# Four chained graph layers over 16 groups: the first two and the last two groups run side by side, with new step orders on all engines

## What is computed

```python
x = _layernorm(x + _L0_gnn_ref(x, adj, ...))   # weight = adj * exp(q k^T), divided by its row sum, times v
x = _layernorm(x + _L1_gnn_ref(x, adj, ...))   # three times adj @ (x @ W) + b, relu after the first two
x = _layernorm(x + _L2_gnn_ref(x, adj, ...))   # hypergraph: H = (adj != 0), up to 512, relu, layer norm, down to 256
x = _layernorm(x + _L3_gnn_ref(x, adj, adj, ..., 128))   # attention, 8 heads of 32, scores * (adj + adj), softmax
```

## Time and profile before

| | |
|---|---|
| median of 3 runs | 1045.72 us (1045.23 to 1046.17) |
| profiled execution, first to last instruction | 1044.3 us; what lies around it is 1.4 us of the median |
| PE busy | 1010.7 us (97%) |
| DVE busy | 840.8 us (81%) |
| ACT busy | 642.8 us (62%) |
| POOL busy | 491.3 us (47%) |

### The profile page before, as it was taken

How to read it: one execution, slowest core, us unless ns; L and a number is a source line. 1 busy time by engine, 2 the same in 40 slices (tenths; PEclk the granted TensorE clock), 3 DMA queues, 4 the chain that set the end, 5 groups by cost and what they waited for, 6 DMA issues and landing times.

```text
span 1044.3 us, 21534 instructions
## 1 busy us (share of the span) xinstructions
PE 1010.7 (97%) x8292; PEld 901.9 (86%) x8292; DVE 840.8 (81%) x2246; ACT 642.8 (62%) x1739; POOL 491.3 (47%) x298
## 2 busy tenths in 40 slices
PE   9799999999999999999999999999999999998876
...
PEclk8999999999999999999999999999999999999998
...
DMA packets 15078, 39.14 MB, mean 37 GB/s; under 512 B 1792, under 2 KB 1792, under 8 KB 14848
## 3 DMA queue, kind: packets, MB, share of 16 engines
...
## 4 chain that ended last, share of the span: by engine, by line
PE 91%; DVE 4%; ACT 2%; issue 1%; POOL 1%; DMA 0%; POOLq 0%; DVEq 0%; SPq 0%
PE ps L465 83%; PE ps L775 5%; PE ps L716 1%; DVE pr L1236 1%; PE ps L702 1%; PE ps L646 1%; DVE mx L1241 1%; ACT pr L935 1%; DMA pr<-in_weights 0%; DVE x L1120 0%; POOL pr L1368 0%; DVE st L1058 0%; POOL rstd L1322 0%; DVE den L1250 0%; ACT up_high L912 0%
## 5 line engine op out<-in xcount | busy, mean ns | idle before, releaser
L1368 POOL TENSOR_TENSOR pr<-pr,den 128x1024 f32<-128x1024 f32 x64 | 132.0, 2064 | 68.7 <-DVE den L1256 68.5
L935 ACT ACTIVATE pr<-pr,mx 128x128 f32<-128x128 f32 x384 | 149.3, 407 | 6.6 <-DVE mx L1241 6.6
L1322 POOL TENSOR_TENSOR rstd<-var,neg_half 128x4 f32<-128x4 f32 (+1 forms) x84 | 74.4, 886 | 96.5 <-DVE var L1069 94.8
L1347 POOL TENSOR_TENSOR x<-x,rows 128x1024 f32<-128x1024 f32 x16 | 38.0, 2376 | 169.4 <-PE ps L465 169.4
L1074 DVE TENSOR_SCALAR x<-x,mv,rstd 128x256 f32<-128x256 f32 x256 | 90.5, 414 | 23.1 <-POOL rstd L1322 23.1
L1357 POOL TENSOR_TENSOR hv<-hv,neg_half 128x2 f32<-128x2 f32 x32 | 22.4, 701 | 161.8 <-DVE hv L1202 161.8
L1058 DVE BATCH_NORM_STATS2 st<-x 128x6 f32<-128x256 f32 x256 | 92.6, 412 | 1.9
L1236 DVE TENSOR_TENSOR pr<-ps,adjB 128x1024 f32<-128x1024 f32 x64 | 75.4, 1219 | 13.9 <-PE ps L465 13.9
L935 ACT ACTIVATION_READ_ACCUMULATOR pr<-pr,mx 128x1 f32 x384 | 78.8, 205 | 0.0
L929 ACT ACTIVATE qkT<-ps,biases 128x512 f32<-128x512 f32 x64 | 39.7, 689 | 62.7 <-PE ps L465 62.4
L1352 POOL TENSOR_TENSOR up_rest<-upT,up_high 128x1024 fp32r<-128x1024 f32 x32 | 77.7, 2430 | 0.0
...
## 6 DMA issues: line engine op xcount, KB each, us to landing
xT<-in_xT SPq DMA_DIRECT2D x16, 512.0 KB, 5.0
x<-in_x SPq DMA_DIRECT2D x16, 512.0 KB, 3.7
out_x<-x SPq DMA_DIRECT2D x32, 256.0 KB, 2.0
adjT<-in_adjT SPq DMA_DIRECT2D x16, 256.0 KB, 5.2
adjB<-in_adj SPq DMA_DIRECT2D x16, 256.0 KB, 5.0
pr<-in_weights SPq DMA_DIRECT2D x2, 512.0 KB, 6.0
qkT<-in_weights SPq DMA_DIRECT2D x1, 1024.0 KB, 11.8
...
```

Of the source, the lines that this page charges most:

```text
L935: act.activation(pr[:, b, k, :], pr[:, b, k, :], ACT.Exp, bias=mx[:, b, k:k + 1], accum_out=den[:, b, 0, k:k + 1]).then_inc(exp_ready, 1)
L1322: pool.tensor_tensor(rstd[i][:, bs], var[i][:, bs], neg_half[:, bs], ALU.pow).then_inc(rstd_ready[i], len(pairs))
L1368: pool.tensor_tensor(pr[:, b], pr[:, b], den[:, b, 1, :].unsqueeze(2).broadcast_to([P, HEADS, P]), ALU.mult).then_inc(pr_ready, 1)
```

## The change

Four things, made together.

- **Two groups side by side at both ends.** Group 1 runs its stage A beside group 0's, in tiles that stages B and C don't use yet (`begun(g)`, names ending in `_b`) and in the upper four PSUM banks (`low`). Group 15 runs its stages B and C beside group 14's, in tiles of stage A (`ended(g)`, names ending in `_z`) and in the lower four banks (`up4`). To place one tile over another, `sb` now gives out addresses itself.
- **Stage A a group further ahead.** In the loop A is group t, its last steps (`T`, from `gcn_3s` on) t-1, B t-2 and C t-3; steps called `N` prepare group t+1. `x1` and `gmT` have two tiles. There are 11 turns.
- **Tiles saved.** `p0T` is now made in place in `e0`, `gm` in `hT`; `gram_turn` therefore waits for `z2_rest` as well.
- **New orders** in all three tables on all five engines. Only two `keep_busy` steps are left, those at the very start.

```diff
-            for t in range(3, NG - 1):
+            for t in range(T0, NG - T1):
                 for stage, name in SCHEDULE[who]:
-                    steps[name](t - "ABC".index(stage))
+                    steps[name](t - BACK[stage])
...
+T0, T1 = 4, 1
...
+BACK = {"N": -1, "A": 0, "T": 1, "B": 2, "C": 3}
...
+        def low(g):
+            return 4 if begun(g) else 0
+
+        def up4(g):
+            return 0 if ended(g) else 4
...
+        xT_b = over("xT_b", [P, C, N4], home["sqs"]); x_b = over("x_b", [P, GB, D], home["fT_high"])
...
+        pr_z = over("pr_z", [P, GB, HEADS, P], home["up_high"]); qkT_z = over("qkT_z", [P, 2 * C, N4], home["upT"])
...
             sp.dma_start(xT[:], A["xT"][0]).then_inc(xT_in, 16)
+            sp.dma_start(xT_b[:], A["xT"][1]).then_inc(xT1_in, 16)
             sp.dma_start(pr_flat[:, q:v], columns("Wv0T", "Wv0T")).then_inc(wv_in, 16)
...
-            sp.dma_start(adjB[:], A["adj"][0]).then_inc(adjB_in, 16)
             sp.dma_start(adjT[1][:], A["adjT"][1]).then_inc(adjT_in[1], 16)
+            sp.dma_start(x_b[:], A["x"][1]).then_inc(x1_in, 16)
...
                 pe.wait_ge(x_high_ready, g + 1)
+                if g == 1:
+                    pe.wait_ge(down_ready, 1)
...
-    "POOL": [("x_rest0", 0), ("att_t", 0), ("x0_stats0p", 0), ("x0_stats1p", 0), ("x_rest", 0), ("x0_bias", 0),
...
+    "POOL": [("att_t", 0), ("att_t", 1), ("x_rest", 0), ("x_rest", 1), ("x0_stats0p", 0), ("x0_stats1p", 0),
...
+                if g == 1:
+                    pool.wait_ge(x1_in, 16)
+                else:
+                    pool.wait_ge(x_in, 16 * max(g, 1))
```

More of the change, by code:

```diff
@@ L19 @@
+import math
 from contextlib import ExitStack
@@ L62 @@
 PROLOGUE = {
-    "PE": [("keep_busy2", 0), ("keep_busy5", 0), ("set_att", 0), ("set_vec", 0), ("att_t", 0), ("att_t_rest", 0),
-        ("att_v0", 0), ("set_down", 0), ("att_v1", 0), ("att_scores", 0), ("set_wo", 0), ("att_out", 0), ("gram", 0),
[3 rows of a table removed]
-        ("att_t_rest", 1), ("att_v0", 1), ("att_v1", 1), ("att_scores", 1), ("hyper_x", 0), ("att_out", 1),
[13 rows of a table removed]
-    "DVE": [("set_rep", 0), ("set_att", 0), ("rest_att", 0), ("set_vec", 0), ("rest_Wv0T", 0), ("set_reps", 0),
-        ("incidence", 0), ("rest_W2", 0), ("rest_WupT", 0), ("set_down", 0), ("rest_Wv3T", 0), ("att_exp", 0),
[21 rows of a table removed]
@@ L105 @@
-    "ACT": [("x_high", 0), ("high_att", 0), ("high_Wv0T", 0), ("att_v0", 0), ("high_WupT", 0), ("high_W3", 0),
[19 rows of a table removed]
-    "SP": [("att_scores", 0), ("att_out", 0), ("gcn_3a1", 0), ("att_scores", 1), ("att_out", 1), ("gcn_3a1", 1),
-        ("att_scores", 2), ("att_out", 2), ("mha_scores1", 0), ("x3_norm1", 0), ("x3_norm0", 0)],
+    "PE": [("keep_busy2", 0), ("keep_busy5", 0), ("set_vec", 0), ("set_att", 0), ("set_down", 0), ("att_t", 0),
+        ("att_t_rest", 0), ("att_v0", 0), ("att_v1", 0), ("att_scores", 0), ("set_wo", 0), ("att_out", 0), ("att_t", 1),
+        ("att_t_rest", 1), ("att_v0", 1), ("gram", 0), ("att_v1", 1), ("att_scores", 1), ("gcn_ax", 0), ("att_out", 1),
[18 rows of a table added]
```

511 lines of the change are left out of this document (317 added, 194 removed), and 333 rows, old and new, of tables (EPILOGUE, PROLOGUE, SCHEDULE).

## The result

| | before | with the change |
|---|---|---|
| median (range, runs) | 1045.95 us (1045.23 to 1046.54, 4) | 1090.81 us (1089.53 to 1092.23, 4) |
| span of the profiled execution | 1044.3 us | 1090.4 us |
| PE busy | 1010.7 us (97%) | 1012.5 us (93%) |
| DVE busy | 840.8 us (81%) | 897.2 us (82%) |
| mean granted clock of PE | 0.990 | 0.983 |

The changed kernel is slower: ratio 1.0428, 95% interval 1.0416 to 1.0440. The forecast was 1041.5 us with a range of 1027 to 1051. PE does the same work, and DVE has 56 us more of it by the profile, though its instructions are nearly the same in number (2252 against 2246).

A forecast was written before the change was run, and what follows sets the result against it. PE, busy for 97% of the span, was taken as the bound at 60.90 us a turn. 1044.3 + 0 (loop) + 1.5 (start) − 5.7 (end) = 1040.1, plus 1.4 for the median: 1041.5 us, range 1027 to 1051.

The forecast's parts named there:

- The loop: 0.: Loop turns: same products, PE at 60.90 us a turn, DVE 10 below, so no change, ±2 us in all.
- The start: +1.5.: Start: att_out of group 0 5.8 us later, 8.7 recovered, 4.4 of new waits; ends -3 and +8.
- The recovery of 8.7 us: Start: of about 11 us of PE waits, fillers and low clock, group 1's products can fill 8.7.
- the first rival: Start: POOL's queue is not recovered, 8.1 us lost, 1048.1 us, or 1051.3 with 3.2 of low clock; chance 0.20.
- The end: -5.7.: From hyper_out of group 13 to the end: 129.8 us against 135.5; ends -20 and +8.
- I take the low clock as lasting as long as before: PE's clock: low stretches as long as before despite 40 filler products removed; otherwise 3.2 us more at the start.
- The rival on the slow side: Start: the loss from POOL's queue is not recovered, whole kernel at 1045 to 1051 us; chance 0.20.
- The rival of a shorter loop: Loop: the new order drops small gaps, 1 us a turn, 11 in all, about 1030 us; chance 0.04.

The follow-up runs named there:

- e7: e6 with POOL steps in the prologue's second half moved away from DVE's sums of squares, and DVE's x1_norm of group 2 later: 1056.7 us.
- e6: The changed kernel with some loop steps of POOL, DVE and ACT moved, plus the start's order of the kernel before: 1060.7 us.
- e12: e10 with two prologue moves: ACT's mha_exp2a of group 0 ahead of up_out3, POOL's x1_bias of group 0 ahead of x1_stats0p: 1038.6 us.
- e10: e7 with POOL's loop steps reordered, DVE's x0_norm of group 15 earlier, and sixteen filler products at two waits behind group 13: 1042.2 us.

## Why the prediction was wrong, and where it was right

- **"The loop: 0."** This step failed, and with it the sign: +29.4 us in ten turns. It compared the products of a turn, DVE's load and the waits of PE in the old trace, and took for granted that an instruction keeps its length in another order. POOL's order in the loop was not walked at all; POOL is busy for half the time there. The prediction named the turn of 60.90 us as a thing to look at, but had a case only for a shorter one. The old trace had a sign of it. Timeline, POOL and then DVE, of the kernel before:

```profile
308.85 2.77 POOL L1368 TENSOR_TENSOR pr<-pr,den 128x1024 f32<-128x1024 f32 x1 [1.90 <-DVE den L1256]
```

```profile
308.69 1.17 DVE L1245 TENSOR_TENSOR pr<-pr,mx 128x1024 f32<-128x1024 f32 x1
```

The division takes 1.90 us elsewhere and 2.77 here, where it starts 0.16 us behind an instruction of DVE with two inputs in SBUF; it is 0.87 us longer, and that one had 1.01 us left. This row and the rule in the Trainium skill, "SBUF", section "Who interferes with whom", together would have given a price for each long POOL instruction placed right behind an `x_stats`.
- **"The start: +1.5."** The part up to PE was right: `x_b`'s sum was foreseen for 21.0 and started at 20.59, `att_t_rest` for 25.8 and started at 25.78. `att_out` of group 0 came 8.4 us later than before (33.94 against 25.55), not 5.8. PE's clock was low again from 27 to 30 (0.50), which is 1.5 of the 2.6 us; the rest stays open. The recovery of 8.7 us did not come in this order of steps. At `gram_turn` of group 4 the loss had grown to 18.2, by waits of 3.21, 2.28, 1.71, 1.82 and 1.78 us. e7 shows three of them to be meetings of POOL and DVE in whole or in part. e6 gives the first piece, 9.1 us by the medians and 10.2 by the start of the profiled executions, which lies within the price of the first rival (8.1 and up to 3.2 of clock); e7 gives another 3 to 4. In e12, with these waits gone or shorter, the start stands at -3.4.
- **"The end: -5.7."** From `hyper_out` of group 13 to the end 132.8 us were measured, 129.8 predicted, 135.5 with nothing gained. The sum left out the clock: "I take the low clock as lasting as long as before". With two of the three low stretches gone, the same part of e10 takes 129.6 us, so the work was sized right. The path to that number was not quite it, and part of the hit is luck: from 58.7 to 85.3 us behind this `hyper_out` DVE was to be busy without a gap, and it is for 19.2 of these 26.6 us (21.5 in e10). Over the span the mean granted clock is 0.983 against 0.990, at most 18.5 us lost against 10.4 (0.017 x 1090.4 and 0.010 x 1044.3). With sixteen filler products put back, e10 has -6.1. The rule in the Trainium skill, "TensorE: Matmul & The Clock Gate", section "HAM oscillation — how this bites in real kernels", that waits between bursts bring the clock down, was right here; the prediction weighed it for the start alone, at 3.2 us, and behind the first 27 us alone the low stretches of the change up to 205 us cost 8.2 at most (1.5 from 27 to 30, and the three at the end of this text). What it said of the old trace holds for one of its two rows: at 1014.77 PE had waited for 2.48 us, but in the 5.80 us ahead of 10.8 it was busy for 5.04, and no wait there was longer than 0.67.
- **The chances.** The rival on the slow side had the first piece of the start right and was 40 us too near. No case had a loss inside the loop, where a small one counts eleven times. The sum without it, 1.5 - 5.7 = -4.2, has the sign of what the change gives in e12, which also has the start's old order, four filler steps and the mended meetings: -3.4 - 6.1 + 1.0 in the loop = -8.5 us of span. The rival of a shorter loop read 86% for the weight loads, which is the share of the whole span; in the loop it was 720.83 of 800 us, 90%, and no version of the change came below 61.0 us a turn.
